# One attention-and-experts kernel: the written-out order of its four engines is laid anew

## The reference, cut to what matters

```python
Q, K = ctx @ Wq.T, ctx @ Wk.T
sim = (sum of head products Q K^T) / (sqrt(16) * 4)          # 256x256 a batch
threshold = 76th largest of each row of sim
A = sigmoid(sim) * (sim >= threshold)
A = (A + A.T) / 2
g = sigmoid(gamma_raw)
x = x + (1 - g) * layernorm(x) + g * A                        # x1 in the kernel
z = layernorm(x)
w, idx = top_2(softmax(z @ gate_w.T))                         # of 8 experts
y = sum over the 2 experts of w * (silu(z @ w1[e].T) * (z @ w3[e].T)) @ w2[e].T
y += (silu(z @ ws1.T) * (z @ ws3.T)) @ ws2.T                  # shared expert
out = x + y
```

## Time and profile before

| | |
|---|---|
| median of 3 runs | 113.53 us (113.2, 114.8, 113.53) |
| span of the profiled execution | 111.5 us |
| what the median has beyond that span | 2.0 us |
| TensorE busy | 102.9 us of the span (92%) |
| mean granted TensorE clock | 0.985 of full |

### The profile page before, as it was taken

The page is one execution under the profiler, slowest core; times in us unless marked ns, Lnnn a source line. Parts: engine busy times, 40 slices in busy tenths (PEclk is TensorE's granted clock), DMA queues, the critical chain, the costliest instruction groups (busy, mean ns, idle before and its releaser), DMA issues.

```text
span 111.5 us, 2502 instructions
## 1 busy us (share of the span) xinstructions
PE 102.9 (92%) x816; PEld 100.5 (90%) x816; DVE 84.4 (76%) x276; ACT 61.7 (55%) x155; POOL 70.4 (63%) x141
## 2 busy tenths in 40 slices
PE   6899709889999999999999999999999999999990
PEld 6699608778999999999999999999999999999990
DVE  6689899899998789867659979759418979365731
ACT  4179999989669856289691245243513352052400
POOL 4047788894975887899898591697028550465500
PEclk9999997699999999999999999999999999999999
DMA  2699995000003700000029000010483004520002
GB/s 40 135 341 370 343 374 163 3 0 3 0 0 96 281 9 0 3 0 6 3 47 309 21 9 0 32 62 0 111 263 104 6 3 154 228 94 0 0 0 94
DMA packets 8158, 10.33 MB, mean 93 GB/s; under 512 B 1936, under 2 KB 6544, under 8 KB 8144
## 3 DMA queue, kind: packets, MB, share of 16 engines
q1 hardware_dynamic: 7776, 10.13, 28.6%
q10 hardware_dynamic: 368, 0.04, 0.3%
HBM read 9.09 MB, written 1.08 MB: 91 GB/s over the span
## 4 chain that ended last, share of the span: by engine, by line
PE 78%; POOL 8%; DVE 5%; ACT 4%; issue 2%; POOLq 0%
PE ps_h L1407 23%; PE ps_u L1407 22%; PE ps_y L1435 20%; PE ps_a L1435 3%; PE ps_c L1354 3%; PE ps_u L1280 3%; ACT qkT L577 2%; PE ps_b L1337 1%; DVE near L970 1%; PE ps_a L1325 1%; PE ps_h L1289 1%; POOL rs L371 1%; DVE st L870 1%; DVE left L962 1%; DVE z L1060 1%
## 5 line engine op out<-in xcount | busy, mean ns | idle before, releaser
L452 POOL TENSOR_TENSOR gc<-prod,weights 128x512 f32<-128x512 f32 x16 | 25.9, 1634 | 15.3 <-DMA weights<-gates 9.3
L699 ACT ACTIVATE sil<-ps_h 128x512 f32<-128x512 f32 (+1 forms) x20 | 10.9, 552 | 16.1 <-PE ps_h L1407 16.1
L710 ACT ACTIVATE g_hi<-gc 128x512 fp32r<-128x512 f32 x16 | 10.1, 630 | 15.9 <-POOL gc L452 15.9
L1435 PE MATMUL ps_y<-dn_hi,g_hi 128*128 128x256 f32 x63 | 17.9, 284 | 0.0
L1435 PE MATMUL ps_y<-dn_hi,g_lo 128*128 128x256 f32 x63 | 17.7, 281 | 0.0
L1435 PE MATMUL ps_y<-dn_lo,g_hi 128*128 128x256 f32 x63 | 17.7, 281 | 0.0
L1136 DVE TENSOR_TENSOR g_lo<-gc,g_hi 128x512 fp32r<-128x512 f32 x16 | 13.8, 862 | 2.5 <-ACT g_hi L710 2.1
L1407 PE MATMUL ps_h<-z_hi,up_hi 128*128 128x256 f32 x70 | 14.7, 291 | 0.0
L1124 DVE TENSOR_TENSOR prod<-sil,ps_u 128x512 f32<-128x512 f32 x16 | 10.8, 679 | 4.9 <-ACT sil L699 3.2
L1407 PE MATMUL ps_h<-z_hi,up_lo 128*128 128x256 f32 x70 | 14.0, 281 | 0.0
L1407 PE MATMUL ps_u<-z_hi,up_hi 128*128 128x256 f32 x70 | 14.0, 281 | 0.0
(11 more groups left out here) (210 smaller groups left out, 250.3 us busy)
## 6 DMA issues: line engine op xcount, KB each, us to landing
weights<-gates SPq DMA_DIRECT2D x8, 512.0 KB, 4.5
x_sb<-in_x SPq DMA_DIRECT2D x4, 256.0 KB, 6.0
up_raw<-in_w1t SPq DMA_DIRECT2D x4, 256.0 KB, 5.9
up_raw<-in_w3t SPq DMA_DIRECT2D x4, 256.0 KB, 6.0
dn_raw<-in_w2t SPq DMA_DIRECT2D x4, 256.0 KB, 6.2
out_x<-fin SPq DMA_DIRECT2D x3, 256.0 KB, 2.1
out_x<-fin SPq DMA_DIRECT2D x2, 128.0 KB, 1.7
ctx_sb<-in_ctxT SPq DMA_DIRECT2D x1, 192.0 KB, 4.6
```

What stands on the lines that cost most here:

```text
L452: nc.gpsimd.tensor_tensor(gc[k % 2][:, :].rearrange("p (n t q) -> p n t q", n=2, t=T), prod[s][:, :].rearrange("p (n t q) -> p n t q", n=2 ...
L699: nc.scalar.activation(sil[i % 2][:, :w], ps_h[i % 2][:, :w], ACT.Silu).then_inc(silu_ready, 1)
L710: nc.scalar.activation(g_hi[s][:, :], src[:, :], ACT.Copy).then_inc(ghi0_ready if s == 0 else ghi_ready, 1)
L1435: last = nc.tensor.matmul(dst[:, t * D:(t + 1) * D], g[s][:, tok], w[:, e, :], start=(s == 0 and first and m == 0), stop=(s == SLOTS - 1 a ...
```

## The change

Almost only the order of calls in the four lists changes. No instruction of the computation is added or removed. The fillers of TensorE go from 36 to 45 calls (72 to 90 instructions). One wait is added: `residual1(3)` writes the buffer of x1 that batch 0 used, and now waits for batch 0's `residual2`.

The head of the other lists, and the added wait:

```diff
 GpSimd
+            make_ranks()
             make_ones()
             make_spans()
             make_halves()
+            deviation0()
+            spans0()
             make_ident()
-            deviation0()
-            make_ranks()
-            spans0()
             norm1(0)
-            lower_up(0, 0)
-            make_routing_consts()
             find_hits(0)
             steps(1)
+            lower_gate()
             norm1(1)
-            lower_down(0)
-            lower_gate()
             norm2(0)
-            find_hits(1)
+            lower_up(0, 0)
             lower_up(0, 1)
             lower_up(2, 0)
+            find_hits(1)
+            steps(2)
             lower_up(2, 1)
             add_masked(1)
-            steps(2)
+            lower_down(0)
+            lower_down(1)
+            make_routing_consts()
             norm2(1)
...
 ScalarE
             copy_q0()
+            tanh_gamma()
             tanh_first()
             copy_qk(1)
             copy_qk(2)
-            tanh_gamma()
+            copy_qk(3)
             lean_first()
-            copy_qk(3)
             lean_second()
-            upper_up(0, 0)
             lean_last()
             copy_scores_summed()
+            upper_up(0, 0)
+            upper_up(0, 1)
+            upper_up(1, 0)
             sigmoid(0)
+            upper_gate()
+            upper_up(1, 1)
+            upper_up(2, 0)
+            upper_up(2, 1)
             upper_down(0)
-            sigmoid(1)
-            upper_up(0, 1)
-            upper_gate()
-            upper_up(1, 0)
-            upper_up(1, 1)
             first_balance(1)
             second_balance(1)
             last_pivot(1)
             copy_scores(2)
-            upper_down(1)
-            upper_up(2, 0)
-            upper_up(2, 1)
-            upper_up(3, 0)
             high_z(0)
             copy_scores(3)
...
 VectorE, inside residual1(b)
+                if b >= 3:
+                    dve.wait_ge(fin_ready, T * (b - 2))
 VectorE
             narrow0(0)
+            narrow0(1)
             gamma_parts()
-            narrow0(1)
...
             add_masked0()
+            residual1(0)
             lower_up(1, 0)
-            residual1(0)
             lower_up(1, 1)
+            norm2_first()
             count_above(1)
-            norm2_first()
+            score_stats(2)
+            low_z(0)
             drop_above(1)
             take_near(1, 0)
             take_near(1, 1)
             read_hits(1)
-            low_z(0)
             select(1)
-            score_stats(2)
-            route_a(0)
             gate_values(0, 0)
-            residual1(1)
-            low_g(0, 0)
-            route_b(0)
             gate_values(0, 1)
             lower_up(3, 0)
+            residual1(1)
             lower_up(3, 1)
+            route_a(0)
+            low_g(0, 0)
             gate_values(0, 2)
             score_stats(3)
+            route_b(0)
             gate_values(0, 3)
...
             select(3)
             gate_values(2, 1)
...
             gate_values(3, 1)
+            low_g(2, 4)
+            gate_values(3, 2)
+            gate_values(3, 3)
             low_g(3, 0)
             residual2(2)
             low_g(3, 1)
             low_g(3, 2)
             gate_values(3, 4)
             low_g(3, 3)
             low_g(3, 4)
```

More of the change, by code:

```diff
@@ L513, in _ @@
             lower_up(4, 1)
+            steps(3)
+            find_hits(2)
             norm1(2)
             gate(0, 1)
-            find_hits(2)
             gate(0, 2)
-            gate(0, 3)
-            steps(3)
             add_masked(2)
-            lower_down(1)
             lower_down(2)
             norm2(2)
+            lower_down(3)
+            gate(0, 3)
             gate(0, 4)
-            lower_down(3)
-            lower_down(4)
             norm1(3)
             find_hits(3)
+            lower_down(4)
             gate(1, 1)
@@ L754, in _ @@
             normed1(1)
[L755 removed]
+            upper_down(1)
+            sigmoid(1)
             silu(0, 0)
[L757 to L759 removed]
+            upper_up(3, 0)
             silu(0, 1)
[L761 to L762 removed]
             upper_up(3, 1)
[L764 removed]
             upper_up(4, 0)
             upper_up(4, 1)
+            first_balance(2)
+            silu(0, 2)
+            high_g(0, 0)
+            second_balance(2)
+            tanh_logits(0)
+            silu(0, 3)
+            normed2(1)
             high_z(1)
[L768 to L770 removed]
             last_pivot(2)
+            sigmoid(2)
+            upper_down(2)
+            upper_down(3)
+            upper_down(4)
             silu(0, 4)
             silu(1, 0)
[L774 to L782, removed]
             first_balance(3)
             second_balance(3)
+            silu(1, 1)
+            normed1(2)
+            sigmoid(3)
+            silu(1, 2)
             last_pivot(3)
+            high_g(0, 1)
+            high_g(0, 2)
+            silu(1, 3)
+            tanh_logits(1)
             normed2(2)
[L787 removed]
+            high_z(2)
             silu(1, 4)
[L789 removed]
+            high_g(0, 3)
             high_g(0, 4)
@@ L814, in _ @@
             high_g(2, 4)
+            silu(3, 2)
             high_g(3, 1)
-            high_g(3, 2)
             silu(3, 3)
             silu(3, 4)
+            high_g(3, 2)
             high_g(3, 3)
@@ L1220, in _ @@
             gate_values(1, 1)
+            norm1(3)
             gate_values(1, 2)
             residual1(2)
+            route_a(1)
             route_b(1)
+            low_g(0, 1)
             low_g(0, 2)
+            low_z(2)
             gate_values(1, 3)
-            low_z(2)
-            norm1(3)
+            count_above(3)
+            drop_above(3)
             gate_values(1, 4)
@@ L1230, in _ @@
             low_g(0, 3)
+            gate_values(2, 0)
             route_a(2)
-            count_above(3)
+            route_b(2)
+            take_near(3, 0)
+            take_near(3, 1)
             low_g(0, 4)
-            drop_above(3)
-            take_near(3, 0)
-            gate_values(2, 0)
+            read_hits(3)
+            select(3)
             gate_values(2, 1)
-            take_near(3, 1)
+            gate_values(2, 2)
+            residual2(0)
+            residual1(3)
             low_g(1, 1)
-            read_hits(3)
             low_g(1, 2)
-            select(3)
-            residual2(0)
-            gate_values(2, 2)
-            residual1(3)
             low_g(1, 3)
-            route_b(2)
             low_g(1, 4)
+            low_z(3)
             gate_values(2, 3)
             gate_values(2, 4)
-            low_z(3)
+            residual2(1)
             low_g(2, 0)
-            residual2(1)
             gate_values(3, 0)
+            low_g(2, 1)
             route_a(3)
-            low_g(2, 1)
             route_b(3)
@@ L1493, in _ @@
             up(1, 3)
-            down(0, 1)
             up(1, 4)
             transpose_z(2)
+            down(0, 1)
             down(0, 2)
+            logits(2)
             up(2, 0)
-            logits(2)
             up(2, 1)
+            up(2, 2)
+            sum_hits(3)
             down(0, 3)
             down(0, 4)
-            sum_hits(3)
-            up(2, 2)
+            transpose_masked(3)
             up(2, 3)
+            up(2, 4)
+            transpose_z(3)
             down(1, 0)
-            transpose_masked(3)
-            up(2, 4)
             down(1, 1)
             down(1, 2)
-            transpose_z(3)
             down(1, 3)
-            up(3, 0)
             down(1, 4)
             logits(3)
+            up(3, 0)
             up(3, 1)
```

59 lines of the change are left out of this document (25 added, 34 removed).

## The result

| | before | changed |
|---|---|---|
| median | 113.42 us (4 runs) | 120.37 us (4 runs, 119.53 to 120.56) |
| ratio of the times | | 1.058, 95% interval 1.0515 to 1.065 |
| span of the profiled execution | 111.5 us | 118.7 us (the other three: 118.5, 118.5, 117.6) |
| TensorE busy | 102.9 us | 108.4 us |

From the `up` function on, the same code stands two lines further down: up is L1409, down L1437, low_g L1138, gate_values L1126, transpose_masked L1327, transpose_z L1339, a filler L1282, the first up L1376.

A forecast was written before the change was run, and what follows sets the result against it. Bound by TensorE, full from z_lo's end at 26.07 us; 1.95 + 0.2 (work) - 0.2 - 0.3 (stalls) = 1.65 us gained, a span of 109.85, and with 2.0 around it 111.9 us; range 111.0 to 113.4.

The forecast's parts named there:

- Stalls in the dense stage: TensorE's waits under the new order after the head: 0.2 us at select(3) plus 0.3 us in the tail.
- select(3): Batch 3's mask step on VectorE, behind low_g(0,4) and beside gate(1,2): 0 to 0.5 us lost, 0.2 taken.
- the tail: Last slot: low_g(3,2) collides with gate(3,3), so gate(3,4) and its low half come late; 0.3 us, bounds 0 and 1.0.
- eight margins: Dense-stage meeting points where TensorE's inputs were forecast ready just ahead of it, said to be below 1 us each.
- B: Rival: dense-stage margins too thin, more VectorE collisions with GpSimd, 1 to 1.5 us lost; 112.6 to 113.8 us, chance 0.20.
- The start of the dense stage: Batch 0's z and z_lo come earlier; last third of up(0,0) at 24.15, not 26.12: 1.95 us gained, bounds 1.3 and 2.3.
- VectorE fills the time with both lower_up: Head: VectorE runs both lower_up to about 20.6 us while GpSimd's root, ending at 20.95, sets z's start.
- My first paragraph: What bounds the kernel: TensorE full for 83 us after the head; time is that stage's start, its work and new stalls.
- the fillers: TensorE's keep_warm(13) and keep_warm(16): 3.2 and 3.9 us at full clock, costing nothing or 0.1 us.
- rival D: Clock falls before 17 us, so fillers run at 0.198 us and delay the mask and z_hi: 116.0 us, chance 0.05.
- GpSimd's root at 20.95: Head: batch 0's root ends at 20.95 in place of 21.81 us, 0.85 us earlier, as lower_up(0,0) and lower_down(0) leave.

The follow-up runs named there:

- e4: Old head (the kernel before, up to batch 1's transpose_masked) joined to the changed kernel's dense order: 121.47 us, ratio 1.070.
- e5: Changed kernel with route_b(2) on VectorE moved from ahead of take_near(3,0) to behind residual1(3): 117.71 us, ratio 1.038.
- e6: Changed kernel with the old tail: high_g(3,2) ahead of silu(3,3) on ScalarE, gate_values(3,3) behind low_g(3,2) on VectorE: 119.04 us, ratio 1.045.
- e3: Changed kernel's head up to TensorE's transpose_masked(1), joined to the old dense order: three runs 119.6 to 119.8 us, one 116.51; no ratio given.
- e7: Changed kernel with the edits of e1, e5, e6 and e8 together: 116.17 us, ratio 1.025.
- e8: Changed kernel with the old start (as e1), and GpSimd's lower_up(0,0) made to wait for batch 0's z: 120.08 us, ratio 1.056.
- e10: e7 plus low_g(0,1), low_g(0,2) ahead of route_a(1), gate_values(2,2) behind residual1(3), gate(0,2) behind add_masked(2): 118.66 us, ratio 1.043.
- e2: Kernel before with the changed start alone (keep_warm(4), make_ranks ahead of make_ones): 114.81 us, ratio 1.008.
- e9: Kernel before with low_z(0) earlier, sum_hits(1), transpose_masked(1), upper_up(3,0) moved, two fillers dropped: 113.41 us, ratio 0.999.
- e1: Changed kernel with the old start: keep_warm(5) for keep_warm(4), make_ranks back behind deviation0: 120.02 us, ratio 1.058.

## Why the prediction was wrong

**The step that failed** is "Stalls in the dense stage": 0.2 us for select(3), with bounds of 0 and 0.5, and 0.3 for the tail, with bounds of 0 and 1.0. Measured are 4.54 us, in five places; e4 shows them without the new head, e5 and e6 take three of them away by undoing queue positions, and e3, with the old order, has none of the five. Of the eight margins I had written down, three gave way: down(0,1), 0.5 us; transpose_z(3), 0.5; and gate_values(2,1) against up(2,3), where I had the margin at zero but named the wrong reader: transpose_masked(3) came too late, 1.29 us. down(0,4) (0.90) and the last slot (1.16) weren't in the list; the last is a little above the tail's upper bound. In the middle the walk failed because it used the duration that an instruction has alone. It priced contention for low_g only, at 1.1 us, and took the small instructions of select and route at 0.2. In the trace th_below took 0.88, ex 1.22, comb 1.04 and kth_pick 1.65 us. The trace of before had held the warning: in its route_b(3), ex took 1.21 us beside a gate, at a place where nobody waited. VectorE's queue is serial, so each such microsecond pushes all that stands behind it, and the margins of 0.5 us were gone before the stall that showed. That is read from the rows: no run takes the stretching away and leaves the order, and e5 shows that the order alone, changed, is enough to be rid of two stalls. In the tail I had forecast the stretched low_g(3,2), but not that gate_values(3,3), moved ahead of low_g(3,0), would keep VectorE idle for 5.45 us and with it gate(3,3) (e6). The rival that fits is B, margins too thin; I gave it 0.20 and up to 1.5 us lost, a third of what came.

**Mis-sized: "The start of the dense stage", -1.95 us.** Measured +0.76. Against e7, where the last third starts at 24.41, the changed kernel's 2.47 us are three parts. z starts 1.42 later; of these, 0.9 to 1.0 come with the slow first scores, as e3 and e6 show against e7, and 0.4 to 0.5 I haven't placed. z takes 0.80 longer beside lower_up(0,0), which I saw move behind the root without asking what runs beside z; e8 shows this cause. And the half clock holds the last third for a further 0.25. The start I hadn't costed at all, taking a filler less at the front for nothing; how much of the slow first scores is due to it stays open, since e5 has them fast with the same start. With the start and z undone the term is -1.71 in e7 and -1.73 in e10, and -1.01 in e8, where the first scores were slow all the same. So my durations for the rest held within 0.3 us where they were fast. "VectorE fills the time with both lower_up" also had a price: GpSimd's root took 1.01 us in place of 0.72.

**And a gain at the head needn't come through.** My first paragraph said that the time is the start of the dense stage plus TensorE's work. That holds where all engines shift together: e2's start, 0.75 us later at the last third, cost about 1 us at the end. Where only TensorE's start moves, it is taken back: e9's 1.02 us and e8's 0.8 us of z changed no time, since batch 1's hit and z hang on VectorE and GpSimd. The view of the chain misled here: it shows TensorE without a gap from 26.1 us on, and not that the other engines were a few tenths behind it.

**Right:** the fillers. 26 took 3.15 us and 32 took 3.74, 0.12 each, and none made a mask or a transpose late; rival D, half clock among the fillers, didn't come. The half clock came later, from 26.0 to 29.4 us (granted 0.50 over 26 to 29), and in one of the four runs. **Wrong in the small:** GpSimd's root at 20.95 (22.69; 21.29 in e1). I had z's statistics ready 0.5 us before GpSimd would ask for them; the row of var waits 0.19 us for mv. Three slips of counting: the list of margins has seven below 1 us, not eight (down(1,3) has 1.1); 111.9 is 1.4% below 113.53, not 1.5%; and the changed kernel's runs have 1.9 us outside their span, not 2.0.

**What stays open:** 0.7 us of the 7.14, the 1.1 us of e7's loss that its gaps don't hold, what makes the first scores slow in one execution and not in the next, and which line of the start makes it more frequent, if one does.

## What to carry to other kernels

Where one engine is full and four queues are written out by hand, "slack" of the others is the margin at each meeting point, not their idle share: VectorE was busy 75% of the span, and still an order that put route_b(2) ahead of take_near(3) cost 2.3 us. When walking a new order, lay the durations of VectorE beside GpSimd's. For each VectorE instruction with two tensor inputs in SBUF that starts while GpSimd runs a long tensor-tensor, take the time until that one ends, however small it is, and for a tensor-scalar such as z, too. One with an input in PSUM, a maximum or a reciprocal kept its own time here. And before working out what an earlier start brings, look at what the second batch's chain hangs on: a gain at the head that this chain didn't follow was given back within 10 us in e9.

## What I hadn't expected of the hardware

**Contention goes by the partner's length, not by one's own.** The tile of kth_pick in the changed kernel (duration in ns, min/median/max):

```profile
L975 DVE SCALAR_TENSOR_TENSOR kth_pick<-above,count,near x8: 211/229/1645, 16.8 to 71.5; 128x16 f32<-128x16 f32 x8
```

Sixteen columns took up to 1645 ns, as long as GpSimd's 512 beside it; before, the longest was 306. th_below and z are of one tensor input and were stretched, too (0.17 to 0.88 us; 0.41 to 0.81 each). Not every instruction is. Beside gates and GpSimd's other long tensor-tensors, prod and z_lo (one input in PSUM) took 0.66 to 0.69 us, the maxima of 128x256 0.41 to 0.42 and the reciprocal of 128x16 0.25, as they do alone. The Trainium skill, "GPSIMD Engine Reference", section Key points, says that GpSimd shares its SBUF interfaces with VectorE and contends with instructions of two SBUF inputs or in a 2-port mode. The trace agrees for kth_pick, ex, comb and g_lo; for z and th_below no run here shows which mode they ran in. How long it takes, the rows show: until 0.03 us after the partner's end for the instructions of 16 columns, 0.15 for z and 0.54 for g_lo.

**It goes the other way, too.** GpSimd's root, two columns wide, took 1.01 us beside VectorE's lower_up and 0.72 without.

**The first products.** The scores' first two took 1.19 us in five of the twelve profiled executions and 0.67 or 0.68 in the others. Four of the five have four fillers ahead of them, one (e8) has five; and e5, with four, has 0.67. The granted clock reads 1.00 over 2 to 10 us in e5 and in e8 alike, so it doesn't show this difference.
